# Row transfers of a four-layer graph network: two halves of tiles over 125 partitions in place of 112 and 13 partitions

## The reference

```python
edge_index = jnp.stack([src, dst])
x = _layernorm(x + _L0_gnn_ref(x, edge_index, ...))                 # two SAGE convolutions
x = _layernorm(x + _L1_gnn_ref(x, ..., edge_weight, src, dst, 10))  # 10 diffusion steps on rows 0..255
x = _layernorm(x + _L2_gnn_ref(x, src, dst, ...))                   # edge attention and feed-forward
x = _layernorm(x + _L3_gnn_ref(x, edge_attr_4, edge_attr_32, edge_index, ...))
```

## Time and profile before

| | |
|---|---|
| median of three runs | 3475.71 us (3473.17 to 3476.80) |
| profiled execution | 3477.83 us, of it 3475.8 us from its first to its last instruction (the span) |
| busy: PE, PE weight loads | 2504.5 us (72%), 1283.3 us (37%) |
| busy: DVE, ACT, POOL | 2036.7 us (59%), 1270.5 us (37%), 1152.8 us (33%) |
| chain that ended last, by engine | PE 40%, DVE 22%, issue 10%, POOL 10%, DMA 8%, ACT 7%, SPq 2% |
| moved by transfers that SP issues | 217.00 MB, 20.9% of 16 DMA engines' span |
| moved by POOL's gathers and scatters | 82.99 MB, 9.5% |
| mean granted PE clock | 0.834 of full speed |

### The profile page before, as it was taken

The page is one execution under the profiler, slowest core; times in us unless marked ns, Lnnn a source line. Parts: engine busy times, 40 slices in busy tenths (PEclk is TensorE's granted clock), DMA queues, the critical chain, the costliest instruction groups (busy, mean ns, idle before and its releaser), DMA issues.

```text
span 3475.8 us, 29135 instructions
## 1 busy us (share of the span) xinstructions
PE 2504.5 (72%) x9170; PEld 1283.3 (37%) x9170; DVE 2036.7 (59%) x4008; ACT 1270.5 (37%) x1839; POOL 1152.8 (33%) x844
## 2 busy tenths in 40 slices
PE   5789889898897459890356666298887765887665
PEld 2344445454454325350211111144445332343343
DVE  3578888888877522346533333646564775676433
ACT  2887777677754301211222222001101112435121
POOL 1535344353544652306025555202101212211122
PEclk8889999999998779995578887699886887788777
DMA  6222323233232153237345555502101111111111
GB/s 178 78 77 90 105 82 94 88 101 106 83 95 69 43 159 107 72 95 192 124 118 153 142 153 146 173 5 57 50 12 42 48 36 53 49 34 34 35 45 44
DMA packets 214873, 301.24 MB, mean 87 GB/s; under 512 B 98738, under 2 KB 99126, under 8 KB 213373
## 3 DMA queue, kind: packets, MB, share of 16 engines
q1 hardware_dynamic: 109813, 217.00, 20.9%
q0 software_dynamic: 104960, 82.99, 9.5%
HBM read 175.01 MB, written 160.09 MB: 96 GB/s over the span
## 4 chain that ended last, share of the span: by engine, by line
PE 40%; DVE 22%; issue 10%; POOL 10%; DMA 8%; ACT 7%; SPq 2%; DVEq 0%; POOLq 0%; ACTq 0%
PE bank L1756 6%; PE bank L833 6%; PE bank L279 6%; POOL arena L899 4%; PE bank L1982 4%; POOL arena L1387 4%; ACT RD L402 3%; PE bank L295 2%; PE bank L2113 2%; DVE lst L870 2%; PE bank L271 2%; DMA arena<-y_table,ids 2%; PE bank L787 2%; DVE arena L886 2%; ACT arena L841 2%
## 5 line engine op out<-in xcount | busy, mean ns | idle before, releaser
L279 PE MATMUL bank<-arena 128*125 128x512 f32 x640 | 320.2, 659 | 169.0 <-DVE arena L561 126.8
L899 POOL DMA_INDIRECT arena<-x_table,idd x120 | 162.4, 1353 | 819.0 <-DVE arena L886 306.7
L1387 POOL DMA_INDIRECT arena<-y_table,ids x180 | 228.0, 1266 | 300.2 <-DMA y_table<-arena 248.1
L647 POOL TENSOR_TENSOR arena<-arena,rowv 125x512 f32<-125x512 f32 x80 | 112.3, 1437 | 608.0 <-DVE arena L583 570.4
L1416 PE MATMUL bank<-arena 125*125 125x512 f32 x360 | 209.8, 714 | 123.2 <-DMA arena<-y_table,ids 123.0
L833 PE MATMUL bank<-arena 128*125 128x512 f32 x640 | 283.0, 601 | 8.2 <-DVE arena L1312 7.5
L841 ACT ACTIVATE arena<-bank 128x500 f32<-128x500 f32 x225 | 124.1, 587 | 447.5 <-PE bank L813 236.7
L295 PE MATMUL bank<-arena 128*125 128x512 f32 x640 | 278.9, 593 | 1.3 <-ACT arena L385 1.3
L279 PEld LDWEIGHTS bank<-arena 128*125 128x125 f32 x640 | 131.7, 212 | 344.3 <-issue 177.0
L1574 DVE SCALAR_TENSOR_TENSOR arena<-arena,v,bank 125x512 f32<-125x512 f32 x180 | 134.6, 748 | 205.3 <-PE bank L1416 197.5
L846 ACT ACTIVATE lsr<-lsr 125x4 f32<-125x4 f32 x60 | 12.3, 204 | 596.9 <-DVE lsr L875 596.9
(11 more groups left out here) (359 smaller groups left out, 5087.7 us busy)
## 6 DMA issues: line engine op xcount, KB each, us to landing
y_table<-arena SPq DMA_DIRECT2D x36, 896.0 KB
p_table<-arena SPq DMA_DIRECT2D x25, 896.0 KB
z_table<-arena SPq DMA_DIRECT2D x25, 896.0 KB
x_table<-arena SPq DMA_DIRECT2D x25, 896.0 KB
arena<-x_cols SPq DMA_DIRECT2D x20, 1000.0 KB, 6.4
arena<-x SPq DMA_DIRECT2D x20, 896.0 KB
out<-arena SPq DMA_DIRECT2D x20, 896.0 KB
arena<-x_table SPq DMA_DIRECT2D x5, 896.0 KB
```

The lines of the kernel that those rows point to most:

```text
L279: i = nc.tensor.matmul(b[0:P, :], xT[:, k, j * P:(j + 1) * P], W1r[:, k, :], start=k == 0, stop=k == KC - 1)
L899: nc.gpsimd.indirect_dma_start(out=dst, out_offset=None, in_=table, in_offset=bass.IndirectOffsetOnAxis(ap=idx, axis=0), bounds_check=limi ...
L1387: nc.gpsimd.indirect_dma_start(out=V1[0:P, t, :], out_offset=None, in_=Yd[i % 2], in_offset=bass.IndirectOffsetOnAxis(ap=ids[:, 2, t:t + 1 ...
```

## The change

Every group that the changed functions move is cut in another direction. Both transfers now span all 125 partitions, and each takes two of the four tiles: 500 KB each, with pieces of 4 KB side by side in SBUF and of 2 KB in a table. Bytes, number of transfers, semaphores and their counts stay, and so does every wait.

```diff
+HALVES = slice(0, TG // 2), slice(TG // 2, TG)
@@ sp_rows
-            sp.dma_start(Z[par][0:HI], src[0:HI]).then_inc(A[f"x_in{par}"], 16)
-            sp.dma_start(Z[par][HI:P], src[HI:P]).then_inc(A[f"x_in{par}"], 16)
+            for h in HALVES:
+                sp.dma_start(Z[par][:, h, :], src[:, h, :]).then_inc(A[f"x_in{par}"], 16)
@@ sp_tables
-                sp.dma_start(dst[0:HI], rows4[0:HI]).then_inc(done, 16)
-                sp.dma_start(dst[HI:P], rows4[HI:P]).then_inc(done, 16)
+                for h in HALVES:
+                    sp.dma_start(dst[:, h, :], rows4[:, h, :]).then_inc(done, 16)
@@ sp_out
-            sp.dma_start(dst[0:HI], O[0:HI]).then_inc(C["out"], 16)
-            sp.dma_start(dst[HI:P], O[HI:P]).then_inc(C["out"], 16)
+            for h in HALVES:
+                sp.dma_start(dst[:, h, :], O[:, h, :]).then_inc(C["out"], 16)
@@ store
-            sp.dma_start(dst[0:HI], rows4[0:HI]).then_inc(s, 16)
-            sp.dma_start(dst[HI:P], rows4[HI:P]).then_inc(s, 16)
+            for h in HALVES:
+                sp.dma_start(dst[:, h, :], rows4[:, h, :]).then_inc(s, 16)
@@ load
-            sp.dma_start(rows4[0:HI], src[0:HI]).then_inc(s.s, 16)
-            sp.dma_start(rows4[HI:P], src[HI:P]).then_inc(s.s, 16)
+            for h in HALVES:
+                sp.dma_start(rows4[:, h, :], src[:, h, :]).then_inc(s.s, 16)
```

## The result

| | before | after |
|---|---|---|
| median (lowest to highest) | 3474.44 us (3471.79 to 3476.8) | 3569.59 us (3561.02 to 3580.43) |
| profiled execution, span | 3477.83, 3475.8 us | 3561.02, 3559.0 us |
| mean granted TensorE clock | 0.834 | 0.828 |

The ratio is 1.0276, 95% interval [1.0244, 1.0307]: 95.9 us slower by the ratio (the two medians are 95.2 apart), where 100.2 were forecast. The profiled execution of after is its fastest, so the two traces differ by only 83.2 us.

What follows compares the result with a forecast made beforehand. The chain of waits was taken to bound the kernel (PE 40%, DVE 22%, transfers 8%). Terms 11.2 + 33.6 + 15.7 + 0 + 8.9 + 30.8 = 100.2 us gave 3576 us, range 3510 to 3655.

Steps and rivals of the forecast that it cites:

- A group takes 9.0 us: Data time of a row group on five engines, against 3.4 us before: a lone group is delayed 5.6 us.
- Node loop 0: Node loop's steady part: slower transfers stay covered by slack, costing 0 unless a group takes over 12.9 us.
- Start +11.2: Program start: PE's wait for the second x_cols, behind two x groups on the same five engines, grows by 11.2 us.
- Lone waits 33.6: Six waits (records, two last out groups, fifth P, fourth and last X3), each 5.6 us longer: +33.6 us.
- Pairs +15.7: Edge layer 0: five pairs of Z and X1 stores need 18.0 us each, so the queue never empties: +15.7 us.
- Layer 1 start 0: Layer 1's start, where the chain waits for the last gather to drain: 0, ends -10 and +20 us.
- X2 stores +8.9: Two X2 stores in layer 1 delay the segment ends behind them by 8.9 us.
- Layer 1 end +30.8: End of layer 1: slower loads hold back the weights, then five X2 stores take 45 us: +30.8 us.
- No loss: Rival: the shape is spread over all 16 engines after all, a group stays at 3.3 us: 3475 us; 5%.
- Loop-bound: Rival: transfers fill the node loop's step from 12.9 us per group; at 14 us the total is 3830 us; 4%.
- Mostly covered: Rival: groups under 7.6 us or gathers gaining more on free engines; sum 20 to 50 us, 3495 to 3527; 15%.
- longer queues: Rival: layer 1's gathers starve at its start (+50), loads at its end take longer (+45): 3640 to 3700 us; 14%.

Runs made afterwards that it cites:

- loop_halves: Before, with only the node loop's transfers (sp_rows, sp_tables, sp_out) as two tile halves over 125 partitions: 3500.74 us, 1.0073.
- layer1_start_halves: Before, with only layer 1's five X1 loads and two X2 stores ahead of the iterations as halves over 125 partitions: 3477.88 us, 1.0018.
- layer2_first_halves: Before, with only the five X3 stores of layer 2's first loop as halves over 125 partitions: 3487.17 us, 1.0032.
- layer0_halves: Before, with only the stores of edge layer 0 (P, Z, X1) as halves over 125 partitions: 3502.23 us, 1.0069.

## Why the prediction was right, and where it was not

- **Five engines.** Right: share 0.32 in row windows, and the series 64, 120, 200, 256 KB.
- **A group takes 9.0 us.** Right for a lone group: landing 10.6 instead of 4.8 us, +5.8 against 5.6. High for queues: 8.7 us in the pairs of layer 0 (118 GB/s) and 8.0 at the end of layer 1 (128 GB/s).
- **Node loop 0.** Right: step 54.59 us in after, and `loop_halves` is accounted for by start, records and outs.
- **Start +11.2.** Mechanism right, size +8.3: x_cols is issued later (49.6 against 42.7 us) and lands 26.8 us on, against 25.3.
- **Lone waits 33.6.** Records +6.1, outs +5.8 and +6.8, P +5.8, last X3 +5.8, and +5.8 for the fourth X3: 36.1.
- **Pairs +15.7.** Mechanism right: the queue never empties (share 0.32 over the 86 us above, and 0.29 or more in each window of 2 us from 1530 to 1616). The size is 13.6 in after (first Z store at 1529.3, last landing at 1619.3), since a group took 8.7 us and not 9.0. From the fourth X1 on each is issued only when the one before has landed, so these landings, each behind a Z, stand one behind another in the chain (rows above).
- **Layer 1 start 0, X2 stores +8.9.** +6.3 [1.7, 10.8] for both in `layer1_start_halves`. In after the two X2 stores cost 10.0 (first issue to landing of the segment ends: 22.9 us against 12.9) and the part ahead of them gained 4 to 5. The gathers' drain left the chain, and DVE waits for the loads instead:

```profile
1653.42 36.13 DMA arena<-x_table
```


- **Layer 1 end +30.8.** Mechanism right, term mis-sized: +21.3 by the traces. Nine groups at 8 us instead of 9 account for it.
- **Layer 2: the step that failed.** The prediction gave it "the fourth X3 of layer 2 (2561)" and the last X3, 11.2 in all; it took +21.1 in the trace of after. I counted the landings that stood in the chain, and in this loop only one did. But `U2` is one buffer, so DVE waits for the store before in every round; before, those waits were 3 us each and the chain ran over the gathers beside them. The list of waits showed it (12.3 us, four times), and the prediction did not use it. Of the 35.5 us more of waiting there, slack hid some 20 and the loop became about 15 longer, where the prediction had 5.6. The first three landings are 14 to 16 us rather than 10.6, and gathers run beside them (DMA share up to 0.9 where the store alone has 0.32). `layer2_first_halves` brings the rows back alone; its median says 11.1 [7.3, 14.6], above 5.6 too.
- **The sum.** The errors of the end of layer 1 (8 to 9 too much) and of layer 2 (10 too little) cancel. That 100 came so near to 96 is in part luck; it says more for the group time than for each term.
- **Rivals.** No loss: share 0.32, refuted. Loop-bound: refuted for the change, and even with 256 KB on an engine the step stays; no kernel came to the 12.9 us of data per group from which the prediction had the loop pay. Mostly covered, and longer queues: the measured 96 us lies between them. Gathers starved at the start of layer 1: they weren't.

## What to carry to other kernels

In this kernel the partition count of a transfer decided how many engines carried it: look at its share in a window, and cut odd counts into a multiple of 16 and a rest (112 + 13), the small tables' loads included. When a transfer becomes slower, don't count only the landings in the chain; list every wait for that tensor, with single buffers first, because one with 3 us of wait and no slack joins the chain at once. When terms are added, check each against a kernel that changes it alone, since errors cancel in a sum.

## What the runs showed of the hardware

- Engines used by SP's transfers of 112, 100, 125 and 124 partitions: 16, 10, 5, 4 (shares 0.99, 0.63, 0.32, 0.26). A broadcast from DRAM follows the same rule: splitting `rowv` and the keys raised the share from 0.33 to 1.03.
- One engine moved 22.5 KB per us (23 GB/s) by the slope of lone landings, and 128 / 5 = 25.6 GB/s in a queue of stores. It is no constant: five engines that are busy throughout moved 118 GB/s in the pairs of after and 106 in those of `layer0_halves`.
- With few engines, SP itself is blocked in issuing: ten loads took it 41.5 us, ten stores 38.9 (rows above), where an issue alone is 0.3 to 0.5 us. In these two places SP's next duty had to wait for the same transfers anyway. At the start of layer 1 the blocking is in the chain: behind the two X2 stores, SP needs 6.8 us to issue the first segment end, against 0.8 before.
- Unexpected: the iterations of layer 1, untouched, take 364 to 374 us from one trace to another, and the part of layer 2 behind its fifth store 264 to 273, so differences below some 10 us in one stretch of one pair of traces aren't to be read.
